# A DLRM tower with a CIN layer: the leftover products of two groups share one operand, and P's first tile goes through the bank from group 2 on

## The reference

```
for i, (w, b) in enumerate(zip(weights, biases)):
    z = jnp.einsum('bhd,bfd->bhfd', hidden, x).reshape(B, hidden.shape[1] * F, D)
    y = jnp.einsum('bcd,oc->bod', z, w) + b[None, :, None]
    y = jax.nn.relu(y)
    if i != n_layers - 1:
        hidden, direct = (y[:, :size // 2, :], y[:, size // 2:, :])
    else:
        direct = y
    finals.append(direct)
return jnp.concatenate(finals, axis=1).sum(-1)
```

## Time and profile before

| | |
|---|---|
| median of 3 runs | 1061.82 us (1060.72 to 1062.32) |
| the profiled execution | 1062.44 us, of it 1060.6 us from the first to the last instruction (the span) |
| PE busy | 1017.3 us, 96% of the span |
| DVE busy | 947.4 us, 89% |
| POOL busy | 917.9 us, 87% |
| ACT busy | 770.0 us, 73% |
[...]
| DMA | 183.92 MB, mean 173 GB/s |

### The profile page before, as it was taken

The page is one execution under the profiler, slowest core; times in us unless marked ns, Lnnn a source line. Parts: engine busy times, 40 slices in busy tenths (PEclk is TensorE's granted clock), DMA queues, the critical chain, the costliest instruction groups (busy, mean ns, idle before and its releaser), DMA issues.

```text
span 1060.6 us, 11306 instructions
## 1 busy us (share of the span) xinstructions
PE 1017.3 (96%) x3519; PEld 661.0 (62%) x3519; DVE 947.4 (89%) x777; ACT 770.0 (73%) x908; POOL 917.9 (87%) x310
## 2 busy tenths in 40 slices
PE   2399999999999999999999999999999999999999
PEld 1146566566666666666666666666766666666663
DVE  3089999999999999999999999999999999999991
ACT  5047666677878877877778777877787887788772
POOL 6528888799999999999999999999988989899880
PEclk9999999999999999999999999999999999999999
DMA  6498888878878877888778878887776776777630
GB/s 173 96 223 195 186 186 193 183 180 193 190 174 191 187 185 179 191 194 189 176 182 193 187 175 192 193 191 170 168 169 167 171 183 162 166 181 180 161 80 0
DMA packets 140638, 183.92 MB, mean 173 GB/s; under 512 B 55633, under 2 KB 56273, under 8 KB 140450
## 3 DMA queue, kind: packets, MB, share of 16 engines
q1 hardware_dynamic: 135986, 178.93, 72.0%
q0 software_dynamic: 4096, 4.20, 2.7%
q10 hardware_dynamic: 496, 0.06, 0.0%
HBM read 174.66 MB, written 8.39 MB: 173 GB/s over the span
## 4 chain that ended last, share of the span: by engine, by line
PE 64%; DVE 16%; issue 9%; ACT 4%; DMA 2%; ACTq 2%; SPq 1%; POOL 1%; POOLq 0%; DVEq 0%
PE py L723 28%; DVE zf L622 11%; PE py L743 11%; PE py L731 10%; PE py L732 10%; DVE zlB L642 2%; DMA xs<-x_dram 1%; ACTq L502 1%; DVE pzS L631 1%; ACT hid L470 1%; DVE zS L635 1%; ACT hid L469 1%; PE py L762 1%; POOL zl L380 1%; DMA xs<-in_L_rec_w 1%
## 5 line engine op out<-in xcount | busy, mean ns | idle before, releaser
L380 POOL TENSOR_TENSOR zl<-zf,zh 128x2048 fp32r<-128x2048 f32 x178 | 785.5, 4419 | 85.0 <-ACT zh L445 82.5
L622 DVE TENSOR_TENSOR zf<-xs,hid 128x2048 f32<-128x2048 f32 (+1 forms) x256 | 538.6, 2108 | 31.3 <-ACT hid L470 25.6
L723 PE MATMUL py<-zf,wf 128*128 128x512 f32 x944 | 426.9, 592 | 1.2 <-DVE zf L622 1.2
L445 ACT ACTIVATE zh<-zf 128x1536 fp32r<-128x1536 f32 (+1 forms) x184 | 338.2, 1838 | 94.5 <-DVE zf L622 90.5
L731 PE MATMUL py<-zh,wh 128*128 128x512 f32 x736 | 290.5, 395 | 1.5 <-ACT zh L445 1.1
L723 PEld LDWEIGHTS py<-zf,wf 128*128 128x128 f32 x944 | 178.4, 189 | 176.7 <-issue 161.5
L732 PE MATMUL py<-zh,wl 128*128 128x512 f32 x736 | 288.4, 392 | 0.0
L743 PE MATMUL py<-zl,wh 128*128 128x512 f32 x736 | 227.3, 431 | 1.4 <-POOL zl L380 1.4
L743 PEld LDWEIGHTS py<-zl,wh 128*128 128x128 f32 x736 | 138.7, 189 | 66.8 <-issue 36.8
L731 PEld LDWEIGHTS py<-zh,wh 128*128 128x128 f32 x736 | 138.4, 188 | 39.5 <-issue 8.5
L369 POOL DMA_INDIRECT emb<-in_tbl,idx x128 | 132.2, 1033 | 28.8 <-issue 22.6
(11 more groups left out here) (100 smaller groups left out, 608.8 us busy)
## 6 DMA issues: line engine op xcount, KB each, us to landing
xs<-x_dram SPq DMA_DIRECT2D x512, 256.0 KB
xs<-x_dram SPq DMA_DIRECT2D x504, 64.0 KB
x_dram<-emb SPq DMA_DIRECT2D x66, 64.0 KB, 5.6
x_dram<-emb SPq DMA_DIRECT2D x22, 96.0 KB
emb<-in_tbl,idx POOLq DMA_INDIRECT x128
x_dram<-emb SPq DMA_DIRECT2D x4, 384.0 KB
xs<-in_L_rec_w SPq DMA_DIRECT2D x2, 512.0 KB
xs<-in_L_rec_w SPq DMA_DIRECT2D x1, 1024.0 KB
```

What stands on the lines that cost most here:

```text
L380: pool.tensor_tensor(zl[:, q, first:T], zf[:, s, first:T], zh[:, q, first:T].bitcast(F32), ALU.subtract).then_inc(lo["P"], 1)
L445: act.activation(zh[:, q, first:T], zf[:, s, first:T], ACT.Copy).then_inc(hi, 1)
L622: dve.tensor_tensor(zf[:, slot(u), first:T], left[:, first:T], view(right, at, [[0, T - first], [1, N]]), ALU.mult).then_inc(mult, 1)
L723: mm = pe.matmul(y, wf[:, w, h], zf[:, s, h], start=first and h == first_tile, stop=ends and h == T - 1)
```

## The change

- `through_bank`: P in groups 2 to 63, not 44 to 63.
- S is made for two groups at once. Pair 0 is group 0 alone, pair q is groups 2q-1 and 2q. Rows 0 to 63 of the operand belong to the first group, rows 64 to 127 to the second; of each 64, 32 rows carry the negated high part and 32 the low part of that group's 32 rows. `wS` has two halves, each with zeros in the other group's 64 rows, so each group's tail is still one matmul of 128 rows, over the same zS. The weights' rows carry a high and a low part, negated where they meet the negated high part of z.
- For pair q, ScalarE copies xt_pair into pzS (`copy_xt`), VectorE multiplies pzS by x0_pair in place (L631's successor), ScalarE rounds it into zS_high, and VectorE forms zS = pzS * low_rows - zS_high with one scalar_tensor_tensor over 128 rows; low_rows is a column of 0 and 1. These run in even groups g for pair g/2 + 1; copy_xt runs in odd groups.
- SP loads xt_pair in even groups and x0_pair in odd groups, four DMAs each, in the place of load_xt; load_xt_pair waits for copy_xt of the pair before, load_x0_pair for the product of the pair before. In the start, load_x0_pair(1) is added between load_xt_pair(1) and load_xe(0).
- C with a bank tile: its other three tiles are computed first, then lowP, then C's bank tile; ScalarE and TensorE take C's tile 0 last as well. load_xd also waits for the bank tile. copy_x0 waits for P's product, not for S.
- The weights are prepared by some more small operations on VectorE at the start; wSf goes.

```diff
-    return name == "P" and g > 43 or name == "C" and 11 <= g < 43 or name == "D" and 11 <= g < LAST
+    return name == "P" and g > 1 or name == "C" and 11 <= g < 43 or name == "D" and 11 <= g < LAST
 ...
+def pair_groups(q):
+    if q == 0:
+        return 0, 0
+    return 2 * q - 1, min(2 * q, LAST)
+def pair_of(g):
+    return (g + 1) // 2, 0 if g % 2 or g == 0 else 1
 ...
-            def load_xt(k):
-                if k >= 2:
-                    sp.wait_ge(s_mult, k)
+            def load_xt_pair(q):
+                k = pair_groups(q)
+                if k[1] % GC == 0:
+                    sp.wait_ge(x_stored[k[1] // GC], 16 * STORES[k[1] // GC])
+                if q >= 2:
+                    sp.wait_ge(xt_copied, q - 1)
                 for j in range(4):
-                    sp.dma_start(xt[F * j:F * j + F], run_of_rows(k, 16)).then_inc(xt_in, 16)
+                    sp.dma_start(xt_pair[F * j:F * j + F, :], run_of_rows(k[j // 2], 16)).then_inc(xt_pair_in, 16)
+            def load_x0_pair(q):
+                if q >= 2:
+                    sp.wait_ge(s_mult, q)
+                for j in range(4):
+                    sp.dma_start(x0_pair[F * j:F * j + F, :], run_of_rows(pair_groups(q)[j // 2], 0)).then_inc(x0_pair_in, 16)
 ...
+                    if through_bank(("C", k - 2)):
+                        sp.wait_ge(bank_mult, NTH_BANKED["C", k - 2])
 ...
-            load_xt(1)
+            load_xt_pair(1)
+            load_x0_pair(1)
             load_xe(0)
             load_x0(2)
             for g in range(G):
                 if g + 2 < G:
-                    load_xt(g + 2)
+                    if g % 2:
+                        load_x0_pair(g // 2 + 2)
+                    else:
+                        load_xt_pair(g // 2 + 2)
 ...
-            act.activation(wS[:], pzS[:, 0:P], ACT.Copy).then_inc(w_high, 1)
-            act.activation(wSf[:], pzS[:, 0:P], ACT.Copy).then_inc(w_high, 1)
+            act.wait_ge(cleared, 7)
+            for half in range(2):
+                rows = slice(H * half, H * half + H)
+                act.activation(wS[rows, half], pzS[rows, 0:P], ACT.Copy).then_inc(w_high, 1)
 ...
             def copy_x0(k):
                 act.wait_ge(x0_in, 64 * k)
-                act.wait_ge(s_mult, k)
+                if k >= 2:
+                    act.wait_ge(mult, NTH["P", k - 1])
                 act.activation(px0[:], x0, ACT.Copy).then_inc(x0_ready, 1)
 ...
-            def high_s(k):
-                act.wait_ge(s_mult, k + 1)
-                if k >= 1:
-                    act.wait_ge(y1_ready, k)
-                act.activation(zS[:], pzS[:], ACT.Copy).then_inc(s_hi, 1)
+            def copy_xt(q):
+                act.wait_ge(xt_pair_in, 64 * q)
+                act.wait_ge(s_lo, q)
+                act.activation(pzS[:], xt_pair[:], ACT.Copy).then_inc(xt_copied, 1)
+            def high_s(q):
+                act.wait_ge(s_mult, q + 1)
+                if q >= 1:
+                    act.wait_ge(s_lo, q)
+                act.activation(zS_high[:], pzS[:], ACT.Copy).then_inc(s_hi, 1)
 ...
+                if g == 0:
+                    copy_xt(1)
                 high(("A", g))
                 if g + 1 < G:
                     high_bank(("P", g + 1))
-                    high_s(g + 1)
+                    if g % 2 == 0:
+                        high_s(g // 2 + 1)
                     if g + 2 < G:
                         copy_x0(g + 2)
+                if g % 2 and g + 2 < G:
+                    copy_xt(g // 2 + 2)
+                high(("C", g))
                 high_bank(("C", g))
-                high(("C", g))
 ...
+            dve.tensor_tensor(sum16, view(xs, 2048 + 16, [[2 * F + 1, 16]]),
+                              view(xs, 2048 + 16 * (2 * F + 1) + 16, [[2 * F + 1, 16]]), ALU.add).then_inc(w0_doubled, 1)
+            dve.wait_ge(w0_doubled, 4)
+            dve.tensor_copy(pair16[:, 0], sum16).then_inc(w0_doubled, 1)
+            dve.wait_ge(w0_doubled, 5)
+            dve.tensor_tensor(pair16[:, 1], sum16, pair16[:, 0].bitcast(F32), ALU.subtract).then_inc(w0_doubled, 1)
+            dve.wait_ge(w0_doubled, 6)
+            pair16_twice = pair16[:].bitcast(F32).rearrange("p (a w) n -> p a (w n)", a=1).to_broadcast([P, 2, F])
+            dve.tensor_copy(view(zf, 4096 + 544 + F, [[2 * F, 2], [1, F]]), pair16_twice).then_inc(w0_doubled, 1)
+            dve.tensor_scalar(view(zf, 4096 + 544, [[2 * F, 2], [1, F]]), pair16_twice, -1.0, None, ALU.mult).then_inc(w0_doubled, 1)
+            for j in range(4):
+                dve.memset(low_rows[F * j:F * j + F], float(j % 2)).then_inc(cleared, 1)
+            dve.memset(wS[:].bitcast(F32), 0.0).then_inc(cleared, 1)
 ...
-                if first:
+                def bank_tile():
                     if NTH_BANKED[u] > 1:
                         dve.wait_ge(bank_lo, NTH_BANKED[u] - 1)
                     dve.tensor_tensor(pzB[:], left[:, 0], view(right, at, [[1, N]]), ALU.mult).then_inc(bank_mult, 1)
-                dve.tensor_tensor(zf[:, slot(u), first:T], left[:, first:T], view(right, at, [[0, T - first], [1, N]]), ALU.mult).then_inc(mult, 1)
-            def products_s(k):
-                if k >= 1:
-                    dve.wait_ge(xt_in, 64 * k)
-                    dve.wait_ge(s_lo, k)
+                def other_tiles():
+                    dve.tensor_tensor(zf[:, slot(u), first:T], left[:, first:T], view(right, at, [[0, T - first], [1, N]]), ALU.mult).then_inc(mult, 1)
+                if first and name != "C":
+                    bank_tile()
+                other_tiles()
+                if name == "C" and g + 1 < G:
+                    low_bank(("P", g + 1))
+                if first and name == "C":
+                    bank_tile()
+            def products_s(q):
+                if q >= 1:
+                    dve.wait_ge(xt_copied, q)
+                    dve.wait_ge(x0_pair_in, 64 * q)
+                    dve.tensor_tensor(pzS[:], pzS[:], x0_pair[:], ALU.mult).then_inc(s_mult, 1)
                 else:
                     dve.wait_ge(x_spread, T + 2)
-                left, right = (xt, px0[:]) if k >= 1 else (xt_first, x0_first[:])
-                dve.tensor_tensor(pzS[:], left, right, ALU.mult).then_inc(s_mult, 1)
-            def low_s(k):
-                dve.wait_ge(s_hi, k + 1)
-                dve.tensor_tensor(zS[H:P], pzS[H:P], zS[H:P].bitcast(F32), ALU.subtract).then_inc(s_lo, 1)
+                    dve.tensor_tensor(pzS[:], xt_first, x0_first[:], ALU.mult).then_inc(s_mult, 1)
+            def low_s(q):
+                dve.wait_ge(s_hi, q + 1)
+                if q >= 1:
+                    dve.wait_ge(y1_ready, 2 * q - 1)
+                dve.scalar_tensor_tensor(zS[:], pzS[:], low_rows[:], zS_high[:].bitcast(F32), ALU.mult, ALU.subtract).then_inc(s_lo, 1)
 ...
-                    products_s(g + 1)
+                    if g % 2 == 0:
+                        products_s(g // 2 + 1)
                 products(("C", g))
                 if g + 1 < G:
-                    low_bank(("P", g + 1))
-                    low_s(g + 1)
+                    if g % 2 == 0:
+                        low_s(g // 2 + 1)
 ...
-                    if through_bank(u):
-                        pe.wait_ge(bank_hi, NTH_BANKED[u])
-                    for h in range(T):
+                    for h in range(1, T + 1) if through_bank(u) else range(T):
+                        if h == T:
+                            h = 0
+                            pe.wait_ge(bank_hi, NTH_BANKED[u])
 ...
             def tail(k):
-                pe.wait_ge(s_lo, k + 1)
-                pe.matmul(py1[:], wS[:], zS[:], start=False, stop=True).then_inc(y1_ready, 1)
+                q, half = pair_of(k)
+                pe.wait_ge(s_lo, q + 1)
+                pe.matmul(py1[:], wS[:, half], zS[:], start=False, stop=True).then_inc(y1_ready, 1)
```

More of the change, by code:

```diff
@@ L138, in dlrm_tower @@
         wlB = sb("wlB", [P, len(OWN), P], F32R)
-        wSf = sb("wSf", [P, P])
-        wS = sb("wS", [P, P], F32R)
+        wS = sb("wS", [P, 2, P], F32R)
+        pair16 = sb("pair16", [P, 2, 16], F32R)
+        low_rows = sb("low_rows", [P, 1])
         ident = sb("ident", [P, P])
@@ L143, in dlrm_tower @@
         bias1 = sb("bias1", [P, 1])
-        xs = sb("xs", [P, 3 * T + 2, N])
+        xs = sb("xs", [P, 3 * T + 1, N])
+        x0_pair = sb("x0_pair", [P, N])
+        xt_pair = sb("xt_pair", [P, N])
         zf = sb("zf", [P, ZF, T, N])
@@ L150, in dlrm_tower @@
         zS = sb("zS", [P, N], F32R)
+        zS_high = sb("zS_high", [P, N], F32R)
         dir1 = sb("dir1", [P, N])
@@ L170, in dlrm_tower @@
         x0 = xs[:, 3 * T]
-        xt = xs[:, 3 * T + 1]
         xs_flat = xs[:].rearrange("p t n -> p (t n)")
@@ L180, in dlrm_tower @@
         sym = zf_flat[:, 4096:4096 + 512]
-        sym16 = zf_flat[:, 4608:4608 + 128]
+        sum16 = zf_flat[:, 4608:4608 + 16]
+        sym16 = zf_flat[:, 4640:4640 + 128]
```

(15 more changed lines are left out.)

## The result

| | before | after |
|---|---|---|
| median | 1061.79 us (1060.72 to 1062.88, 6 runs) | **1057.84 us** (1057.16 to 1057.96, 6 runs) |
| span of the profiled execution | 1060.6 us | 1056.2 us |
| ratio | | 0.996, 95% interval 0.995 to 0.997 |

What follows compares the result with a forecast made beforehand. TensorE bounds the kernel up to group 43; from tail 47 VectorE's loop holds it back slightly. Terms 7.3 + 6.1 + 1.4 - 0.5 = 14.3 us, from 1061.8 to 1047.5 us, range 1045.0 to 1054.5.

Steps and rivals of the forecast that it cites:

- the forecast's pulse: Tail matmuls, one per group, start 15.02 us apart from group 12 to 63, without the step at 47.
- the named rivals: VectorE becomes the bound, 0.13; late stretch stays held back, 0.15; savings taken back elsewhere, 0.04; slower, VectorE held by POOL, 0.05.
- Part 1, the bank: Groups 2 to 43: P's tile 0 as three fp32r matmuls instead of an fp32 tile on TensorE saves 7.3 us.
- Part 2, the S pair: One S operand for two groups frees 1.33 us of VectorE per two groups; TensorE stays the bound, late stretch gains 6.1.
- The late stretch: Tails 43 to 63: VectorE's shortened loop lets the pace become TensorE's 15.02 us a group, saving 6.1 us.
- the loop of before: Late groups: the chain from A through VectorE and ScalarE to the next A, 15.08 or 15.44 us, holds TensorE back.
- The rival of VectorE held by POOL: The new low_s waits for POOL's operations, 2.3 us in the mean: 48 us above the forecast, 1096; chance 0.05.
- Part 3, the end: TensorE's wait for POOL's low of A(63) disappears as A comes earlier, saving 1.4 us.
- Part 4, the start: Four more x0_pair loads ahead of xe(0) and x0(2) delay B(0), costing 0.5 us, bounds 0 and 2.5.
- C's bank tile last: TensorE takes up C 5 us after its high part is there, and xd's extra wait adds no delay: nothing.

Runs made afterwards that it cites:

- e6: Changed kernel with z moved 96 bytes on by an unused array behind low_rows, restoring the distance of the kernel before (64); 1049.13 us.
- e1: Changed kernel with 32 unused bytes behind low_rows, so z moves 32 bytes on, to distance 0; 1043.87 us, ratio 0.982.
- e11: Changed kernel with weights and z both padded to start at 64 modulo 256 bytes, distance 0; 1044.64 us.
- e7: Kernel before with 64 unused bytes ahead of ident, z at a multiple of 256, distance 128; 1065.83 us.
- e9: Changed kernel with weights and z both padded to start at multiples of 2048 bytes, distance 0; 1044.52 us.
- e10: Kernel before with 192 unused bytes ahead of ident, giving distance 0; 1058.72 us, ratio 0.997.
- e4: e1 with P through the bank only in groups 44 to 63, as before the change, so the paired S operand alone; 1050.87 us.
- e8: e7 plus P through the bank from group 2 and C's bank tile last, S still made for every group; 1074.04 us, ratio 1.011.
- e12: Changed kernel with a pad of 40 values, z at a multiple of 256 and weights at 128, distance 128; 1057.43 us.

## Why the prediction was wrong

**The step that failed** is one that the prediction never wrote down as a step: "0.231 us for an fp32r matmul" and "15.02 us a group" were taken from the trace of before and put into the changed kernel as constants. They are the pace at distance 64. The change moves z by 160 bytes modulo 256, to distance 224, where one of `main` costs 0.0044 us more and a group 0.16 us (15.18 against 15.02). By the table of stretches this takes 6.2 us from the forecast between tails 2 and 43 (1.05 gained, 7.3 forecast) and 3.2 between tails 43 and 63 (2.93, 6.1): 9.4 us. The start took 0.6 us more than its term, the end gave 0.2 more: 14.3 - 9.4 - 0.6 + 0.2 = 4.5 us in the two profiled executions, and 4.0 in the medians.

e6, with nothing changed but the placement, has the forecast's pulse exactly and a median of 1049.1, 1.6 above the forecast. Its start was late: tail 1 is at 71.24 in its profile and at 68.58 after. The placement alone isn't why: at distance 0, tail 1 is at 68.60 in e1 and at 70.71 in e11. Most of the difference goes with the granted clock. Timeline of PE behind the wait for the product A(0), in e11 and in e1:
```profile
62.65 2.93 PE L797 MATMUL py<-zf,wf 128*128 128x512 f32 x3 [2.61 <-DVE zf L683]
```
```profile
62.03 3.27 PE L796 MATMUL py<-zf,wf 128*128 128x512 f32 x7 [1.34 <-DVE zf L682]
```
In e6, e7, e9 and e11 this idle time of TensorE is 2.26 to 3.07 us, and from 62 to 66 us the granted clock has a mean of 0.57 to 0.69; in e11 it is 0.50 from 63 to 65 us, and 1.00 again from 66, and of the 2.11 us that tail 1 is later than in e1, 0.62 are there when TensorE starts on A(0) (62.65 against 62.03) and 1.49 come behind it. In the ten other profiles the idle time is 1.2 to 1.9 us and the clock 1.00. The first have tail 1 at 70.71 to 71.24, the others at 68.4 to 69.1.

What should have stood among the rivals: new arrays are declared ahead of the big operands, so these move. None of the named rivals happened. The sign and the mechanisms were right, and the range left out the time because every case in it took the cost of TensorE's own work for known.

**Point by point**, at equal placement where possible (distance 0 on either side: e10 against e11 on one chip, medians 14.1 us apart, and e10 against e1 on two chips, whose kernels before took 1062.68 and 1062.29, medians and spans 14.9 us apart; 14.3 were forecast):

- *Part 1, the bank, 7.3 us*: right, 7.0 by e4 - e1. VectorE's cost for it agrees with e8, 15.60 us a group against 15.6.
- *Part 2, the S pair*: right. Occupied 29.56 us for two groups (29.9 forecast), and TensorE stays the bound even at 14.95 us a group, where A still waits for hid in e1, 0.26 us at 451.04 and at most 0.34 in the middle. The new low_s goes by the value taken: 0.66 us from start to start, not 1.2. The late stretch, 6.1 us: at equal placement tails 43 to 63 take 306.70 in e10 and 299.34 in e1, 7.4 us. It is more than forecast because the loop of before doesn't get faster with TensorE, so a faster TensorE had more to lose to it. In the kernel after, 2.9 us show, for TensorE's own pace had become the slower one (15.18 a group, against 15.33 in the mean of before).
- *The rival of VectorE held by POOL*: not seen. 33 low_s take 739 to 749 ns each, with 0.7 us of waiting in all, while POOL was busy for 574.22 of 615.10 us; POOL was at work beside 31 of them. A VectorE operation with a PSUM operand, an SBUF tensor and an SBUF scalar column isn't held by POOL in this trace, where the rival reckoned 2.3 us for each.
- *Part 3, the end, 1.4 us*: right, 1.6, and no wait of TensorE for POOL there.
- *Part 4, the start, 0.5 us*: mis-sized, 1.08 at tail 2 (1.19 in e1 against e10). Timeline after, DVE's B(0), PE's D(0), ACT's copy of x0(2):

```profile
69.18 6.68 DVE L681 TENSOR_TENSOR zf<-xs,hid 128x2048 f32<-128x2048 f32 x3 [0.84 <-DMA xs<-x_dram]
...
73.72 3.70 PE L795 MATMUL py<-zf,wf 128*128 128x512 f32 x8 [0.90 <-DVE zf L681]
...
70.17 0.60 ACT L471 ACTIVATE px<-xs 128x512 f32<-128x512 f32 x1 [4.05 <-DMA xs<-x_dram]
```

B(0) waits 0.84 us for xe(0), not 0.5, and TensorE, which had no gap there before, waits 0.90 us for D(0), one of VectorE's row of three. x0(2) comes at 70.17, 1.31 us later than in the earlier trace rows. The direction and the queue are those of the prediction; the landing of xe(0) worked out from a mean bandwidth was 0.3 us early. The other 0.2 to 0.3 us were not followed.
- *C's bank tile last, nothing*: C waits nowhere in the quoted rows; it was not run by itself.

**What stays open.** Why the distance counts. TensorE's weight loads run beside its matmuls (PEld has 412.87 us busy in the 615.10 us from 100 to 715.1 in which PE is busy throughout); whether they have a part in it is not shown, as no run took them away. fp32 passes stay at 0.429 us at every distance tried. Distances 32 and 160 weren't run, and at 128 two kernels differ (0.2323 in e7, 0.2332 in e12), so the distance isn't all there is. The late starts of e9 and e11 explain why they are 0.7 us behind e1 only if their other executions, which weren't profiled, have them too. Why A(0) comes later in those four isn't known.

## What to carry to other kernels

A duration read from a trace is that of its placement too: here the same matmul took 0.2269 to 0.2336 us. When an edit declares, drops or resizes anything on chip, list which operands move and by how much before the old durations are used again, and run the edit once more with a pad that restores the old distance: that run (e6) separates the mechanism from the placement. In a kernel whose TensorE is full, try the placement by itself; here 32 bytes of padding gave the changed kernel 14 us, 3.5 times what the change had shown as it stood (the kernel before got 4.0 us from the best distance, e10), and the version with both is the fastest of all (e1, 1043.87 us, 1.8% under the kernel before).

## What the runs showed of the hardware

- The spacing of fp32r matmuls of 128x128 by 512 columns at a granted clock of 1.00 (those of `main`) goes with the distance, in bytes of an SBUF row modulo 256, from the stationary operand to the moving one: 0.2269 us at 0 (five kernels), 0.2290 at 64 (two), 0.2334 at 96, 0.2323 and 0.2332 at 128, 0.2331 at 192, 0.2333 and 0.2336 at 224. From best to worst 3.0%. Pairs of `late` follow it less closely: 0.228 at 0, 0.2297 and 0.2313 at 64, 0.2306 (e7) to 0.2337 at the others. The fp32 pass: 0.429 us throughout. At 0 and 224 (e1 and after) the pace with ScalarE, GpSimd and the DMAs idle is that of the middle (0.227 and 0.234 us in seven intervals).
- A scalar_tensor_tensor over 128x512 with a PSUM operand, a column and an SBUF operand takes 0.74 us on VectorE, a plain tensor_tensor with one PSUM operand 0.69 (742 and 689 ns in the list of groups), with POOL busy beside it.
- After idle times of TensorE of 2.26 to 3.07 us at the start, the granted clock fell to 0.50 in four profiles (0.57 to 0.69 in the mean from 62 to 66 us), and tail 1 came some 2 us later; after 1.2 to 1.9 us it stayed at 1.00 in the ten others.
